# A chain of norms, mixers and experts on one core: Flow's entry reordered, stage changes keyed to the last products, filler moved

## The chip, the core and the metric

The kernel runs on one core of one Trainium2 chip. Its engines are PE (TensorE: matrix products and transposes), DVE (VectorE), ACT (ScalarE), POOL (GpSimd) and SP, which here issues the DMAs. Each engine runs its own instructions in the order in which they are written and waits on semaphores for the others. The metric is the device time of one execution in microseconds; lower is better. The time before is 947.53 us, the median of 3 runs (947.06 to 948.75).

## What is computed

x is 4096 tokens of 128 channels (4 sequences of 1024). Six blocks follow one another, each on the layer norm of x, each added to x:

```python
x = x + 0.5 * ffn0(norm(x))       # stage 1: silu(gate) * up, hidden 384
x = x + time_mixing(norm(x))      # stage 2: a decayed scan over time
x = x + 0.5 * ffn0(norm(x))       # stage 3
x = x + 0.5 * experts(norm(x))    # stage 4: 8 experts, top 2, gelu
x = x + flow(norm(x))             # stage 5: causal "flow" attention, 16 heads of 8
x = x + 0.5 * experts(norm(x))    # stage 6
```

Flow is what the change is mostly about:

```python
q, k = sigmoid(x @ Wq + bq), sigmoid(x @ Wk + bk); v = x @ Wv + bv
sink   = n / sum_d((q + eps) * (cumsum(k) + eps))            # first sum
source = n / sum_d((k + eps) * (cumsum(q) + eps))
con_sink   = sum_d((q + eps) * (cumsum(k * source) + eps)) / n   # second sum
con_source = sum_d((k + eps) * (cumsum(q * sink) + eps)) / n
cs = exp(con_source); comp = cs / cumsum(cs) * n             # third sum
out = (q * sink / n) . cumsum(k (x) v * comp) * sigmoid(con_sink)
out @ Wo + bo
```

## The kernel before

x stays in SBUF as X, 32 tiles of 128 tokens. Each stage runs over 8 chunks (NCH) of four tiles, 512 tokens, pipelined by hand: every engine has its own program text with the same stages, and `stages` strings them together with a wait at each change. FF, TM, MO and FL are the semaphore sets of ffn0, time mixing, experts and Flow.

At a stage change ACT writes the first chunk's normalised input Z "ahead" of the wait. PE then turns it (`turn_chunk`, four 128-wide transposes into a bank of PSUM), and ACT copies the turned tile to SBUF, from where PE multiplies. Before, the wait between the two stages was on `x` of the old stage, which DVE counts up when it has added the stage's last chunk to X (`add_to_x`, L1241); in the text it is, for the change from stage 4 to Flow, `eng.wait_ge(MO.x, NCH + CREDIT)`. The semaphores `down`, `out` and `rT` of the change are PE's own: they count its last transposes or projections of a chunk, which DVE's addition reads. POOL's `ahead` for Flow fills the carries cum1 and cum2 of the sums behind the same wait (L749 to L751).

In Flow the engines go through i = -1 to 8 and work in step i on chunk a = i + 1 (first part), b = i (second part) and c = i - 1 (last part). On PE a step is, in its order: `turned_output`, `states`, `project` of earlier chunks; `turn_chunk(a)`; `second_sum(b)`; `queries_keys(a)`; `values(a)`; a product of 64 columns over cs (third sum, L1898); `first_sum(a)`; the turn of qq (L1916) and more states. In step 0 the order is another: `queries_keys(1)` and `values(1)` come ahead of `second_sum(0)`, since nothing older is there to be done.

A running sum over a chunk is two carried products (the last row of the previous sums, `carried`, 128x512, weight last_row) and two running products (triangular weight until, `running`). second_sum(b) waits for w2, which POOL makes (L830) from DVE's reciprocals of the first sum; DVE's row products (L1452, L1454) read it; from these ACT makes cs (L1082) and a sigmoid (L1088, with a table load ahead of it); PE's small product over cs, DVE's L1482 to L1490, and POOL's kc and qq (L830) follow, then POOL's four key-value products a chunk (L823), which PE's `states` sum up (L1787) and DVE multiplies in `turn` (L1441, L1446) by the query.

`keep_busy(n, to)` issues n fillers, products whose result nobody reads (L1614), into bank `to`. `variances` (L1218 to L1228) is DVE's statistics for the next stage; it is seven small instructions, and at Flow's end it stands between DVE's turns of chunk 6 and of chunk 7.

In the profile the 512-wide and 128-wide fp32 products have two records each, so "x4" of a 512-wide one is two products. All products of Flow that go through `add` carry the line L1780.

## Time and profile before

| | us |
|---|---|
| median of 3 runs (lowest, highest) | 947.53 (947.06, 948.75) |
| the profiled execution's own time | 946.31 |
| its span, first to last instruction | 944.6 |
| PE busy | 868.7 |
| DVE busy | 721.7 |
| ACT busy | 637.8 |
| POOL busy | 589.1 |

The mean granted clock of PE is 0.973 of full speed; in any short stretch it is either 1.00 (2.4 GHz) or 0.50 (1.2 GHz), and a number between them means that the stretch held both. Flow lies between about 510 and 714 us. A row of the timeline gives start, length, engine, source line, operation, output <- inputs, count, and in brackets how long the engine had stood still and what released it. Ends of PE's products are modelled, so the distance from one start to the next is the better measure of what a product costs.

### The profile page before, as it was taken

How to read it: one execution, taken by the hardware profiler on the slowest of the kernel's cores; microseconds unless marked ns; L12 is line 12 of the kernel's file. 1: busy time of each engine (PE TensorE's matmuls, PEld its weight loads, DVE VectorE, ACT ScalarE, POOL GpSimd, SP SyncE). 2: the span in 40 equal slices, each digit the busy share in tenths (PEclk: the TensorE clock that was granted, in tenths of full speed). 3: DMA queues.
4: the chain of work that ended last, by engine and by line, in shares of the span. 5: the costliest groups of instructions: out<-in, count | busy, mean ns of one | idle time of the engine just before them, and what ended most of it. 6: DMA issues, size and time to landing. Idle time of an engine off the chain costs nothing.

```text
span 944.6 us, 14308 instructions
## 1 busy us (share of the span) xinstructions
PE 868.7 (92%) x3982; PEld 465.1 (49%) x3982; DVE 721.7 (76%) x1541; ACT 637.8 (68%) x1153; POOL 589.1 (62%) x560
## 2 busy tenths in 40 slices
PE   7989897787987999999999899999987899999998
PEld 6845463344543444444444456666544444444443
DVE  6956669985676788888865488888886788888874
ACT  3078789977876887788885444444315878788884
POOL 2075775569567766666677355555474766666774
PEclk9999979889999999999999999999989999999999
DMA  8000000000002222211220000000002232123230
GB/s 227 12 1 0 0 1 1 0 1 1 1 1 90 90 91 91 90 55 47 77 91 0 0 2 0 1 1 1 0 1 90 90 93 58 64 89 101 101 102 23
DMA packets 27407, 42.12 MB, mean 45 GB/s; under 512 B 5320, under 2 KB 19036, under 8 KB 27356
## 3 DMA queue, kind: packets, MB, share of 16 engines
q1 hardware_dynamic: 27356, 41.52, 13.8%
q8 instruction: 22, 0.36, 0.2%
q14 instruction: 29, 0.24, 0.1%
HBM read 39.15 MB, written 2.36 MB: 44 GB/s over the span
## 4 chain that ended last, share of the span: by engine, by line
PE 54%; DVE 22%; issue 9%; ACT 8%; POOL 4%; DMA 1%; DVEq 1%; SPq 1%; ACTq 0%; POOLq 0%
PE bank L1780 11%; PE bank L1525 10%; PE bank L1527 9%; PE bank L1526 9%; PE bank L1787 5%; DVE arena L1367 3%; ACT bank L1016 3%; PE bank L1620 2%; POOL rstd L718 1%; PE bank L1747 1%; DVE arena L1414 1%; DVE arena L1413 1%; ACT arena L1008 1%; DVE stats L1199 1%; DVE arena L1441 1%
## 5 line engine op out<-in xcount | busy, mean ns | idle before, releaser
L805 POOL TENSOR_TENSOR arena<-arena 128x512 f16<-128x512 f32 x256 | 293.3, 1159 | 127.0 <-ACT arena L1008 126.2
L1367 DVE TENSOR_TENSOR arena<-bank,arena 128x512 f32<-128x512 f32 x256 | 172.9, 686 | 75.7 <-ACT bank L1016 59.0
L1008 ACT ACTIVATE arena<-arena 128x512 f16<-128x512 f32 x256 | 160.6, 627 | 77.3 <-DVE arena L1367 76.0
L1016 ACT ACTIVATE bank<-bank,eb 128x512 f32<-128x512 f32 x256 | 166.3, 654 | 9.2 <-PE bank L1527 8.7
L1525 PE MATMUL bank<-arena,ew1hi 128*128 128x512 f16 x256 | 97.6, 381 | 1.9 <-DVE arena L1367 1.9
L1526 PE MATMUL bank<-arena,ew1hi 128*128 128x512 f16 x256 | 97.8, 382 | 0.0
L1527 PE MATMUL bank<-arena,ew1lo 128*128 128x512 f16 x256 | 97.7, 382 | 0.0
L1525 PE MATMUL bank<-arena,ew2hi 128*128 128x512 f16 x256 | 97.5, 381 | 0.0
L1526 PE MATMUL bank<-arena,ew2hi 128*128 128x512 f16 x256 | 97.5, 381 | 0.0
L1527 PE MATMUL bank<-arena,ew2lo 128*128 128x512 f16 x256 | 97.5, 381 | 0.0
L830 POOL TENSOR_TENSOR arena<-arena 128x512 f32<-128x512 f32 (+1 forms) x24 | 32.8, 1379 | 86.4 <-DVE arena L1485 65.9
L771 POOL TENSOR_TENSOR arena<-arena 128x512 f16<-128x512 f32 x46 | 52.9, 1161 | 41.1 <-ACT arena L934 41.1
L1787 PE MATMUL bank<-arena,until 128*128 128x512 f32 x128 | 63.7, 621 | 4.3 <-DVE arena L1441 4.2
L1525 PE MATMUL bank<-arena,f0hi 128*128 128x512 f16 x144 | 54.7, 380 | 8.0 <-DVE arena L1270 2.6
L823 POOL TENSOR_TENSOR arena<-arena 128x1024 f32<-128x1024 f32 x32 | 61.7, 1951 | 0.0
L1270 DVE SCALAR_TENSOR_TENSOR arena<-bank,arena 128x512 f32<-128x512 f32 x48 | 33.0, 691 | 28.4 <-ACT arena L943 22.7
L1527 PE MATMUL bank<-arena,f0lo 128*128 128x512 f16 x144 | 54.6, 379 | 0.0
L1526 PE MATMUL bank<-arena,f0hi 128*128 128x512 f16 x144 | 54.6, 379 | 0.0
L920 ACT ACTIVATE Z<-X,nbias,rstd 128x128 f32<-128x128 f32 (+1 forms) x128 | 52.4, 483 | 1.1 <-POOL pool_spare L720 1.1
L1380 DVE TENSOR_SCALAR X<-X,keep,shift (+1 forms) x64 | 51.7, 812 | 0.0
L1441 DVE TENSOR_TENSOR arena<-bank,arena 128x512 f32<-128x512 f32 x64 | 41.9, 684 | 7.5 <-PE bank L1787 7.5
L1199 DVE BATCH_NORM_STATS2 stats<-X 128x6 f32<-128x128 f32 (+1 forms) x188 | 43.6, 286 | 4.7 <-issue 1.5
(278 smaller groups left out, 1850.0 us busy)
## 6 DMA issues: line engine op xcount, KB each, us to landing
arena<-wrows SPq DMA_DIRECT2D x64, 512.0 KB, 5.9
X<-in_L_attn_x_dram SPq DMA_DIRECT2D x8, 256.0 KB, 4.3
out_dram<-X SPq DMA_DIRECT2D x8, 256.0 KB, 5.6
arena<-in_L_ffn_ew_dram SPq DMA_DIRECT2D x2, 512.0 KB, 6.6
arena<-in_L_ffn_ew_dram SPq DMA_DIRECT2D x1, 1024.0 KB
wrows<-arena SPq DMA_DIRECT2D x16, 16.0 KB
arena<-in_L_ffn_gens_dram SPq DMA_DIRECT2D x1, 192.0 KB, 2.6
arena<-in_L_ffn_w_gate_dram SPq DMA_DIRECT2D x1, 192.0 KB, 2.8
```

The source lines that it names most:

```text
L771: pool.tensor_tensor(f0.hlo[:, u, :], f0.h[:, u % 2, :], f0.hhi[:, u, :], ALU.subtract).then_inc(S.hlo, 1)
L805: pool.tensor_tensor(mo.hlo[:, u % 8, :], mo.hw[:, u % 4, :], mo.hhi[:, u % 8, :], ALU.subtract).then_inc(S.hlo, 1)
L823: pool.tensor_tensor(fl.kv[:, b, :].rearrange("p (h m d) -> p h m d", d=HD, m=HD), key.to_broadcast([P, HEADS, HD, HD]), value.to_broadcas ...
L1008: A(mo.hhi[:, u % 8, :], mo.hw[:, u % 4, :], ACT.Copy).then_inc(S.hhi, 1)
L1016: A(bank[MM1_BANK[u]][:, :], bank[MM1_BANK[u]][:, :], ACT.Gelu, scale=1.0 / WS, bias=eb1[:, u:u + 1]).then_inc(S.gelu, 1)
L1199: last = dve.bn_stats(stats[:, bass.ds(tile, 1), :], X[:, bass.ds(tile * P, P)])
L1367: TT(mo.hw[:, u % 4, :], bank[MM1_BANK[u]][:, :], mo.wB[:, p, u // EB, :], ALU.mult)\
L1525: mm(dst, whi, xhi, start=start, stop=False, skip_group_check=True)
L1526: mm(dst, whi, xlo, start=False, stop=False, skip_group_check=True)
L1527: return mm(dst, wlo, xhi, start=False, stop=stop, skip_group_check=True)
L1780: return mm(dst, w, x, start=start, stop=stop, skip_group_check=True)
L1787: mm(bank[5 + h], until[:, :], fl.kv[:, b, h * CH:(h + 1) * CH], start=True, stop=True)\
```

## The change

It has four parts.

1. Flow, step 0 on PE: the carried products of `second_sum` become a function of their own, `second_carry`. In step 0 it stands ahead of `turn_chunk(1)`, in all later steps where it was. `values(1)` moves from ahead of the second sum to behind the small product over cs. Of the fillers around the first two chunks the seven at the end of step -1 and the two of step 0 go, and eight new ones follow `values(1)`. On ACT `value_copy(1)` moves from behind the gates to behind the sigmoid of the second sum, as in the other steps.
2. On PE and ACT (`products=True`) the wait at each of the five stage changes is for the old stage's last product on PE, no longer for DVE's addition to X. POOL's wait ahead of the fills of cum1 and cum2 changes in the same way. Two waits that this needs are put further on: `S.init` in time mixing, and in the first experts stage a wait for FF.x ahead of the gate products, whose bank DVE still reads.
3. Flow, step 7 on PE: the eight fillers ahead of the turn of qq go; four come ahead of the small product over cs, and six behind it.
4. The nine fillers in the first step of an experts stage write bank 2, not bank 0.

```diff
@@ stages @@
-        def stages(eng, ffn0, mixing, experts, flow, ahead):
+        def stages(eng, ffn0, mixing, experts, flow, ahead, products=False):
...
             ahead(TM, 0, 2)
-            eng.wait_ge(FF.x, NCH + CREDIT)
+            if products:
+                eng.wait_ge(FF.down, NCH)
+            else:
+                eng.wait_ge(FF.x, NCH + CREDIT)
             mixing(TM, 0, 2)
...
             ahead(FL, 0, 5)
-            eng.wait_ge(MO.x, NCH + CREDIT)
+            if products:
+                eng.wait_ge(MO.rT, NCH)
+            else:
+                eng.wait_ge(MO.x, NCH + CREDIT)
             flow(FL, 0, 5)
             ahead(MO, NCH, 6)
-            eng.wait_ge(FL.x, NCH)
+            if products:
+                eng.wait_ge(FL.out, NCH)
+            else:
+                eng.wait_ge(FL.x, NCH)
             experts(MO, NCH, 6)
@@ gpsimd, ahead @@
                     if number == 5 and n == 2:
-                        pool.wait_ge(MO.x, NCH + CREDIT)
+                        pool.wait_ge(MO.rT, NCH)
@@ scalar, flow @@
                     if i == 0:
                         gates(a)
-                        value_copy(a)
...
-                    if a < NCH and i != 0:
+                    if a < NCH:
                         value_copy(a)
@@ tensor, mixing @@
             def mixing(S, first, number):
-                pe.wait_ge(S.init, 1)
...
                         o = p * CH
+                        if not lead:
+                            pe.wait_ge(S.init, 1)
                         pe.wait_ge(S.xn, i + 3)
@@ tensor, experts @@
                             if mid:
                                 pe.wait_ge(S.wT, i + 1)
+                            elif number == 4:
+                                pe.wait_ge(FF.x, 2 * NCH + CREDIT)
...
                             if not mid:
-                                keep_busy(9, 0)
+                                keep_busy(9, 2)
@@ tensor, flow @@
-                def second_sum(b):
+                def second_carry(b):
 
                     after(pe, S.snap2, b)
                     after(pe, S.qqT, b)
...
                     for m in range(2):
                         carried(3, m, fl.cum2)
+
+                def second_sum(b):
+
                     pe.wait_ge(S.w2, b + 1)
...
                         project(c - 1)
+                    if i == 0:
+                        second_carry(b)
                     if a < NCH:
                         after(pe, S.pr, a)
                         after(pe, S.snap1, a)
                         turn_chunk(Z, a % 2, S.z, a + 1, S.tr, 1)
                     if i == 0:
-                        keep_busy(2, 5)
                         queries_keys(a)
-                        values(a)
+                    if now and b:
+                        second_carry(b)
                     if now:
                         second_sum(b)
...
                     if a < NCH and i != 0:
                         values(a)
+                    if i == NCH - 1:
+                        keep_busy(4, 1)
                     if now:
                         pe.wait_ge(S.cs, b + 1)
...
                         last.then_inc(S.ccp, 1)
+                    if i == 0:
+                        values(a)
+                        keep_busy(8, 5)
+                    if i == NCH - 1:
+                        keep_busy(6, 1)
                     if a < NCH and i != 0:
                         first_sum(a)
-                    if i < 0:
-                        keep_busy(7, 5)
                     if 0 <= c:
                         states(c, 3)
                     if now:
-                        if i == NCH - 1:
-                            keep_busy(8, 1)
                         pe.wait_ge(S.qq, b + 1)
```

PE's instructions from the end of the first chunk's first sum on, before. last_row is a carried product, until a running one, fw with 256 columns queries and keys, fw with 128 columns values, f0hi a filler, ident with Z the turn.

```order
L1614 MATMUL bank<-f0hi 128x512 x7
L1620 MATMUL bank<-ident,Z 128x128 x4
L1614 MATMUL bank<-f0hi 128x512 x2
L1780 MATMUL bank<-bias_rows,ones 128x512
L1780 MATMUL bank<-fw,arena 128x256 x2
L1780 MATMUL bank<-bias_rows,ones 128x512
L1780 MATMUL bank<-fw,arena 128x256 x2
L1780 MATMUL bank<-bias_rows,ones 128x512
L1780 MATMUL bank<-fw,arena 128x128 x4
L1780 MATMUL bank<-arena,last_row 128x512 x2
L1780 MATMUL bank<-arena,until 128x512 x2
```

Behind them come the first sum of the second chunk (two carried, two running products), the small product over cs and the turn of qq. The same place on PE after the change, up to values:

```order
L1796 MATMUL bank<-arena,last_row 128x512 x2
L1634 MATMUL bank<-ident,Z 128x128 x4
L1796 MATMUL bank<-bias_rows,ones 128x512
L1796 MATMUL bank<-fw,arena 128x256 x2
L1796 MATMUL bank<-bias_rows,ones 128x512
L1796 MATMUL bank<-fw,arena 128x256 x2
L1796 MATMUL bank<-arena,until 128x512 x2
L1796 MATMUL bank<-arena,last_row 128x512 x2
L1796 MATMUL bank<-arena,until 128x512 x2
L1921 MATMUL bank<-arena,until 128x64
L1796 MATMUL bank<-bias_rows,ones 128x512
L1796 MATMUL bank<-fw,arena 128x128 x4
```

The two carried products of the second sum have taken the place of the seven fillers, the running ones stand right behind queries and keys, and values (the last two rows) behind the small product over cs; eight fillers follow them, then the turn of qq.

PE's instructions in Flow's last full step (i = 7), before: states of chunk 6 (until, L1787), the two small products of the third sum (64 columns), states, fillers, the turn of qq, states of chunk 7.

```order
L1787 MATMUL bank<-arena,until 128x512 x2
L1898 MATMUL bank<-arena,until 128x64
L1901 MATMUL bank<-arena,last_row 128x64
L1787 MATMUL bank<-arena,until 128x512 x2
L1614 MATMUL bank<-f0hi 128x512 x8
L1916 MATMUL bank<-ident,arena 128x128 x4
L1787 MATMUL bank<-arena,until 128x512 x2
```

And after the change:

```order
L1803 MATMUL bank<-arena,until 128x512 x2
L1628 MATMUL bank<-f0hi 128x512 x4
L1921 MATMUL bank<-arena,until 128x64
L1924 MATMUL bank<-arena,last_row 128x64
L1628 MATMUL bank<-f0hi 128x512 x6
L1803 MATMUL bank<-arena,until 128x512 x2
L1940 MATMUL bank<-ident,arena 128x128 x4
L1803 MATMUL bank<-arena,until 128x512 x2
```

The fillers have moved from behind the last states of chunk 6 to both sides of the small products.

## Rows read from the trace of the kernel before

**Rows 1.** The page, first part: engine, busy us, share, instructions.
```profile
PE 868.7 (92%) x3982; PEld 465.1 (49%) x3982; DVE 721.7 (76%) x1541; ACT 637.8 (68%) x1153; POOL 589.1 (62%) x560
```

**Rows 2.** The chain of waits, 500 to 560 us: start us, length us, what.
```profile
513.27 7.44 PE bank L1780 x27
...
524.54 10.31 PE bank L1780 x35
```

**Rows 3.** Timeline, change into Flow: start, length, engine, what [idle <- releaser].
```profile
507.99 1.64 ACT L920 ACTIVATE Z<-X,nbias,rstd 128x128 f32<-128x128 f32 x4
...
509.58 0.65 PE L1756 MATMUL bank<-ident,arena 128*128 128x128 f32 x4 [0.92 <-DVE arena L1393]
...
511.02 0.97 PE L1620 MATMUL bank<-ident,Z 128*128 128x128 f32 x4 [0.78 <-DVE X L1241]
...
516.20 1.09 ACT L1055 ACTIVATE arena<-bank 128x512 f32<-128x512 f32 x2 [2.22 <-PE bank L1780]
```

**Rows 4.** Busy time by stretch (PEclk third number from the end).
```profile
511.00:515.00 4.00, 3.98 (x13) 2.64 (x14) 2.04 (x11) 1.88 (x2) 3.76 (x5) 0.57 0.00 0
538.30:542.00 3.70, 3.70 (x14) 3.02 (x15) 1.82 (x3) 0.82 (x2) 3.70 (x3) 0.54 0.00 0
688.50:695.50 7.00, 5.24 (x8) 1.93 (x9) 5.94 (x10) 0.86 (x3) 6.20 (x5) 0.52 0.02 4
560.00:680.00 120.00, 118.02 (x506) 72.06 (x505) 100.60 (x150) 51.75 (x85) 62.71 (x38) 1.00 0.00 1
```

**Rows 5.** The timeline, Flow's second chunk.
```profile
520.54 1.67 PE L1614 MATMUL bank<-f0hi 128*128 128x512 f16 x7
...
523.22 0.63 PE L1620 MATMUL bank<-ident,Z 128*128 128x128 f32 x4 [1.00 <-issue]
...
524.54 0.39 PE L1780 MATMUL bank<-bias_rows,ones 128*128 128x512 bf16 x1 [0.26 <-ACT arena L1073]
...
524.80 1.97 POOL L830 TENSOR_TENSOR arena<-arena 128x1024 f32<-128x1024 f32 x1 [5.92 <-DVE arena L1511]
...
526.91 1.09 ACT L1055 ACTIVATE arena<-bank 128x512 f32<-128x512 f32 x2 [2.42 <-PE bank L1780]
526.92 1.05 PE L1780 MATMUL bank<-fw,arena 128*128 128x128 f32 x8
...
529.53 1.88 PE L1780 MATMUL bank<-arena,until 128*128 128x512 f32 x4
```

**Rows 6.** The timeline, from the wait for qq to the third turn.
```profile
538.16 3.85 POOL L823 TENSOR_TENSOR arena<-arena 128x1024 f32<-128x1024 f32 x2
...
538.25 0.90 PE L1916 MATMUL bank<-ident,arena 128*128 128x128 f32 x4 [3.23 <-POOL arena L830]
...
544.98 0.60 PE L1620 MATMUL bank<-ident,Z 128*128 128x128 f32 x4
```

**Rows 7.** The timeline, Flow's end.
```profile
690.26 3.75 PE L1787 MATMUL bank<-arena,until 128*128 128x512 f32 x4 [1.96 <-DVE arena L1441]
...
691.44 7.67 POOL L823 TENSOR_TENSOR arena<-arena 128x1024 f32<-128x1024 f32 x4
...
694.05 0.69 DVE L1441 TENSOR_TENSOR arena<-bank,arena 128x512 f32<-128x512 f32 x1 [0.89 <-PE bank L1787]
...
695.92 1.35 DVE L1218 TENSOR_TENSOR halfd<-stats 128x24 f32<-128x24 f32 x1
...
697.19 1.99 DVE L1219 TENSOR_TENSOR var<-stats 128x24 f32<-128x24 f32 x1
...
700.76 1.96 PE L1787 MATMUL bank<-arena,until 128*128 128x512 f32 x4 [0.27 <-DVE arena L1441]
```

**Rows 8.** The timeline at the change into the second experts stage.
```profile
714.84 0.66 PE L1620 MATMUL bank<-ident,Z 128*128 128x128 f32 x4 [0.78 <-DVE X L1241]
...
716.78 0.69 DVE L1372 TENSOR_TENSOR arena<-bank,arena 128x512 f16<-128x512 f32 x1
```

**Rows 9.** The timeline at the change into the first experts stage.
```profile
281.50 0.63 PE L1620 MATMUL bank<-ident,Z 128*128 128x128 f32 x4 [0.54 <-ACT Z L920]
```

More of the change, by code:

```diff
@@ L534, in stages @@
             ahead(TM, 0, 2)
-            eng.wait_ge(FF.x, NCH + CREDIT)
+            if products:
+                eng.wait_ge(FF.down, NCH)
+            else:
+                eng.wait_ge(FF.x, NCH + CREDIT)
             mixing(TM, 0, 2)
             ahead(FF, NCH, 3)
-            eng.wait_ge(TM.x, NCH + CREDIT)
+            if products:
+                eng.wait_ge(TM.out, NCH)
+            else:
+                eng.wait_ge(TM.x, NCH + CREDIT)
             ffn0(FF, NCH, 3)
             ahead(MO, 0, 4)
-            eng.wait_ge(FF.x, 2 * NCH + CREDIT)
+            if products:
+                eng.wait_ge(FF.down, 2 * NCH)
+            else:
+                eng.wait_ge(FF.x, 2 * NCH + CREDIT)
             eng.wait_ge(S0.flo, NU // TILES + 1)
@@ L545, in stages @@
             ahead(FL, 0, 5)
-            eng.wait_ge(MO.x, NCH + CREDIT)
+            if products:
+                eng.wait_ge(MO.rT, NCH)
+            else:
+                eng.wait_ge(MO.x, NCH + CREDIT)
             flow(FL, 0, 5)
             ahead(MO, NCH, 6)
-            eng.wait_ge(FL.x, NCH)
+            if products:
+                eng.wait_ge(FL.out, NCH)
+            else:
+                eng.wait_ge(FL.x, NCH)
             experts(MO, NCH, 6)
@@ L1106, in _ @@
             setup()
-            stages(act, ffn0, mixing, experts, flow, ahead)
+            stages(act, ffn0, mixing, experts, flow, ahead, products=True)
         @block.vector
@@ L1932, in _ @@
             setup()
-            stages(pe, ffn0, mixing, experts, flow, lambda S, first, number: None)
+            stages(pe, ffn0, mixing, experts, flow, lambda S, first, number: None, products=True)
 _INS = ["L0_attn_x", "L0_attn_time_decay", "L0_attn_time_first", "L0_attn_time_mix_k", "L0_attn_time_mix_v",
```

## The prediction

> **What bounds the kernel now.** I read the page first: PE is busy 92% of the span [rows 1], so what can be won lies where PE stands still, runs at half clock, or does on the path what could stand elsewhere. Then the chain of waits around Flow's entry (500 to 560 us). It is PE almost throughout; two long pieces, 513.27 to 520.71 and 524.54 to 534.85, hold the first chunk's and the second chunk's products in a row [rows 2]. Between 560 and 680 us PE is busy 118.02 of 120 us [rows 4], so what is saved at the entry is handed on. Then the timeline at the stage change [rows 3], the granted clock by stretch [rows 4], the timeline of the second chunk [rows 5, 6], Flow's end [rows 7] and the other changes [rows 8, 9]. The reader should see in them who is last at each step.
>
> **Stage changes.** Five times PE and ACT no longer wait for DVE's last addition to X but for PE's own last product. It is worth something only where Z, which ACT writes ahead, is already there.
> Into Flow it is: Z is written by 509.63, PE's last transposes end at 510.23, and PE starts the turn at 511.02, after DVE's addition [rows 3]. It can now start at about 510.3: 0.7 us. There is a second gain behind it. The clock was half from 511 to 515 (0.57) [rows 4], after PE had stood for 0.92 and 0.78 us [rows 3]. Without the second pause I expect it to stay full. At full clock the second chunk's step from turn to query-key products takes 524.54 - 523.22 = 1.32 us and from there to ACT's gates 526.91 - 524.54 = 2.37 us [rows 5]. The first chunk's gates so start at 510.3 + 1.32 + 2.37 = 513.99 and not at 516.20 [rows 3]: **2.2 us**, bounds 0.7 (clock falls all the same) and 2.3. What follows the gates was a closed PE chain [rows 2] and moves along. POOL's two fills of the carries move with the same wait and stay ahead of their reader.
> Into the second experts stage the turn at 714.84 could start at most 0.78 us sooner. But the next on the path is DVE's residual of xn at 716.78, which DVE starts without a pause, right behind its own work on the last chunk [rows 8], and that still waits for the last projection: 0. At the other three changes (there are three such rows, one is shown) it is ACT's Z, not DVE's addition, that PE waited for [rows 9]. I take 0 for them, bounds 0 and 0.2 in all. The new wait of the first experts stage's gate products for X stands behind ACT's copy and holds nobody; what is queued behind it on PE is filler.
>
> **The second sum.** From the first to the second chunk the path is turn, query-key products, values, carried products, running products, then DVE's row products, two running products (1.72 us) after 529.53 [rows 5]. The change takes two pieces out: values and the two carried products, together the 2.8 us from 526.75 (values' bias product stands just ahead of the row at 526.92) to 529.53; 1.72 of it is the carried ones, two of 0.86 us, so 1.1 is values. The carried ones go into the hole where PE ran seven fillers (1.67 us from 520.54) while it waited for ACT's copy of the first sum [rows 5]; they take as long, so they are done by 522.4 and the turn still starts at 523.22: cost 0. The running products need w2, which POOL finishes at 524.80 + 1.97 = 526.77 [rows 5]; PE gets there at 526.75. So they start at 526.85 instead of 529.53: **2.7 us** (2.6 to 2.8). This price rests on POOL: any further cut before it is worth nothing.
> Values now stand behind the small product over cs. cs comes 2.7 us earlier as well, since ACT then waits for nothing but DVE's row products. The first sum of the second chunk ends on PE at 534.85 - 2.7, still just where cs is ready. Then PE waited 3.23 us for POOL's qq until 538.25 [rows 6]; that wait is as long as before, since DVE, ACT and POOL between cs and qq are not changed. Values (1.1 us) and eight fillers (1.7 us) lie in that wait, together 2.8, so cover remains, 0.4 us. If it were gone they would cost what they overrun. ACT now copies the values between its sigmoid and its copy of the third sum, so its copy of the first sum comes about 0.6 us later relative to the rest; its reader on PE is the next turn, behind four 512-wide products: 0.
>
> **The clock behind the hole.** After those 3.23 us PE's clock was 0.54 until 542 [rows 4]. The turn of qq, the eight small products and the first states took 538.25 to 544.98 [rows 6]. With the hole filled, PE starts the first states as soon as POOL's first product is there, 538.16 + 1.92 = 540.1, and the second pair when POOL's second ends, 542.0; two products of 0.86 us each end at about 543.8, and the next turn starts then: **1.15 us**, bounds 0.4 and 1.2. Again POOL is the limit. Later the loop is PE's, so it stays.
>
> **Flow's end.** Eight fillers go from behind the last states of chunk 6 to before (4) and behind (6) the small product over cs of the last chunk. The places were pauses (1.96 us in the second [rows 7]); after them the clock was 0.52 from 688.5 to 695.5 [rows 4] and the two products of the states took 3.75 us, where two take 1.88 to 1.96 at full clock [rows 5, 7]. DVE waited 0.89 us there, at 694.05. That wait goes, but buys nothing. DVE's next work is the seven statistics instructions of the next stage, and their first two, on 24 elements a partition, take 1.35 and 1.99 us; they end at 697.27 and 699.18, both just behind a boundary of POOL's four 1.92 us products (691.44 to 699.11) [rows 7]. POOL is not moved, so its last product ends at 699.11 and I let DVE get through behind it as before, at best one instruction sooner: 0.1 us. The Trainium skill states the mechanism (page "SBUF — State Buffer", section "Who interferes with whom"): a DVE instruction with two SBUF inputs contends with a GpSimd instruction that reads SBUF, and the later one waits for the whole of the other. By that rule DVE stays pinned; without it the 0.9 us would come through.
> PE, however, is now early: at full clock its states of chunk 6 end at 692.0, the turn of qq at 692.5, the first states of chunk 7 at 695.1 (they wait for POOL at 693.4), the turned output at 696.9. The next states need DVE's first turn of chunk 7, 700.6 as now (PE started at 700.76) [rows 7]. A pause of 3.7 us opens that the late fillers used to close (0.27 us now). The pause of 3.23 us before 538.25 was followed by half clock for some 3.5 us [rows 4, 6]. The same here makes 3.4 to 3.7 us of PE work take 1.7 us more; DVE's chain of four turns has about 0.35 us of slack for it. Cost **+1.3 us**; bounds -0.9 (clock holds and DVE is not pinned) and +2.8 (half clock for 7 us, as from 688.5).
>
> **The sum.** -2.2 - 2.7 - 1.15 - 0.1 + 1.3 = -4.85; I say -4.8. The span goes from 944.6 to 939.8, the profiled execution's time from 946.31 to 941.5; the median of the three runs is 1.2 above the profiled time, so 947.53 - 4.8 = 942.7. About 0.2% (1.9 us) is what a measurement of this kernel can tell from no change.
>
> **Rivals.**
> 1. Flow's end costs nothing or gains, because the pause falls so that the clock holds, or DVE passes between POOL's products: sum -6.1 to -7.0, time 940.5 to 941.4. For it: one execution does not tell where the fall lands against the pause. Against: the one pause above 3 us in these rows was followed by it at once [rows 4, 6]. 0.2.
> 2. The clock still falls at Flow's entry, since the 0.92 us pause stays: first term 0.7, sum -3.3, time 944.2. 0.14.
> 3. Flow's end costs the double, half clock over two turns: sum -3.3, time 944.2. 0.1.
> 4. It does not do what it says: w2 or qq is later than read, so values or fillers overrun and the second term halves: sum -3.4, time 944.1. 0.04.
> 5. Slower. The entry loses its fillers: PE stands from 522.4 to 523.2 and again from the turn's end to 524.54, and if that drops the clock to half from 524.5 on, each 3.5 us of PE work there costs 1.75. It decides from about 7 us on: with 10 us of work at half clock +5, first term 0.7, third 0, end +2.8: -0.7 - 2.7 + 5 + 2.8 = +4.4, time 951.9. Against: together these pauses are under 1.6 us, with full work between and behind. 0.04.
> My forecast 0.48.
>
> **The numbers.** Forecast 942.7; the range 940.3 to 945.0 takes in rivals 1 to 4 and leaves out the slower one and the far ends of the others. Faster by over 0.2% (below 945.6): 0.93; within 0.2%: 0.04; slower: 0.03.
>
> **What the profile after would show.** Right: PE's turn into Flow right behind its own transposes and a clock of 1.00 up to the gates; DVE's row products of the second sum about 4.9 us earlier than now; no half clock behind the qq wait; at Flow's end DVE's second statistics instruction still ending with a POOL product, PE standing over 3 us before the second states of the last chunk, then half clock. Wrong: the turn waits for Z or the clock drops at 511; the running products start well after the query-key products; DVE's statistics end earlier than POOL's last product, or no half clock after 700, then the gain is larger; the loop between 560 and 680 longer than its present chunk.

## The result and the profile after

The changed kernel takes 942.23 us (median of 4 runs, 940.39 to 943.67), the kernel before 947.60 beside it (median of 4, 947.06 to 948.75): ratio 0.9943, 95% interval 0.9924 to 0.9961, so 5.4 us less (3.7 to 7.2). The forecast was 942.7, -4.8 us, with the range 940.3 to 945.0. The profiled execution after took 943.67 us with a span of 941.9.

PE's busy time fell by 1.5 us, its span in these two executions by 2.7. The page after, against [rows 1]:

```profile
PE 867.2 (92%) x3983; PEld 461.9 (49%) x3983; DVE 722.8 (77%) x1541; ACT 637.5 (68%) x1153; POOL 588.6 (62%) x560
```

At the change into Flow, the timeline after (start, length, engine, what [idle <- releaser]), against [rows 3]:

```profile
511.68 0.66 PE L1772 MATMUL bank<-ident,arena 128*128 128x128 f32 x4 [0.92 <-DVE arena L1407]
512.37 0.69 DVE L1255 SCALAR_TENSOR_TENSOR X<-bank,X 128x512 f32<-128x512 f32 x1 [0.75 <-PE bank L1772]
...
512.40 0.66 PE L1634 MATMUL bank<-ident,Z 128*128 128x128 f32 x4
...
513.15 0.60 ACT L1088 ACTIVATE arena<-bank 128x512 f32<-128x512 f32 x1 [1.42 <-PE bank L1634]
...
516.17 1.08 ACT L1070 ACTIVATE arena<-bank 128x512 f32<-128x512 f32 x2 [1.12 <-PE bank L1796]
```

PE's transposes for DVE start at 511.68 and the turn of the first chunk stands 0.72 us behind them, with no idle time; before it was 1.44 us behind, 0.78 of it waiting for DVE's addition. The gates at 516.17 stand 3.80 us behind the start of DVE's addition (512.37), before 5.93 (510.27 to 516.20): -2.13 us.

The second chunk, against [rows 5, 6]:

```profile
520.52 1.88 PE L1796 MATMUL bank<-arena,last_row 128*128 128x512 f32 x4
...
523.19 0.63 PE L1634 MATMUL bank<-ident,Z 128*128 128x128 f32 x4 [0.80 <-issue]
...
524.77 1.97 POOL L845 TENSOR_TENSOR arena<-arena 128x1024 f32<-128x1024 f32 x1 [4.52 <-DVE arena L1525]
...
526.79 1.98 PE L1796 MATMUL bank<-arena,until 128*128 128x512 f32 x4
...
528.82 1.22 DVE L1466 SCALAR_TENSOR_TENSOR arena<-arena,bank 128x1024 f32<-128x1024 f32 x1 [4.22 <-PE bank L1796]
...
532.43 1.05 PE L1796 MATMUL bank<-fw,arena 128*128 128x128 f32 x8
...
533.32 1.89 PE L1628 MATMUL bank<-f0hi 128*128 128x512 f16 x8
...
535.61 0.66 PE L1940 MATMUL bank<-ident,arena 128*128 128x128 f32 x4 [0.40 <-POOL arena L845]
...
537.52 3.96 PE L1803 MATMUL bank<-arena,until 128*128 128x512 f32 x8 [0.36 <-POOL arena L838]
...
541.32 0.60 PE L1634 MATMUL bank<-ident,Z 128*128 128x128 f32 x4
```

The carried products (last_row, 520.52) fill the hole ahead of the turn, the running ones start at 526.79, just as POOL's w2 is there (524.77 + 1.97 = 526.74). PE's wait for qq is down from 3.23 to 0.40 us, and the third turn follows 28.92 us behind the first, before 33.96.

Flow's end, against [rows 7], and the turn into the second experts stage, against [rows 8]:

```profile
686.60 1.95 PE L1803 MATMUL bank<-arena,until 128*128 128x512 f32 x4 [0.66 <-DVE arena L1455]
...
687.78 7.66 POOL L838 TENSOR_TENSOR arena<-arena 128x1024 f32<-128x1024 f32 x4
...
689.78 1.98 PE L1803 MATMUL bank<-arena,until 128*128 128x512 f32 x4 [0.79 <-POOL arena L838]
...
691.27 0.42 DVE L1232 TENSOR_TENSOR halfd<-stats 128x24 f32<-128x24 f32 x1
...
691.62 1.98 DVE L1233 TENSOR_TENSOR var<-stats 128x24 f32<-128x24 f32 x1
...
693.52 1.98 DVE L1235 SCALAR_TENSOR_TENSOR nmean<-stats 128x24 f32<-128x24 f32 x1
...
696.97 2.66 PE L1803 MATMUL bank<-arena,until 128*128 128x512 f32 x4 [3.42 <-DVE arena L1455]
...
702.59 0.69 DVE L1455 TENSOR_TENSOR arena<-bank,arena 128x512 f32<-128x512 f32 x1 [0.98 <-PE bank L1803]
...
711.96 0.69 DVE L1255 SCALAR_TENSOR_TENSOR X<-bank,X 128x512 f32<-128x512 f32 x1 [2.61 <-PE bank L1796]
...
712.26 0.63 PE L1634 MATMUL bank<-ident,Z 128*128 128x128 f32 x4 [0.34 <-ACT Z L935]
...
714.52 0.69 DVE L1386 TENSOR_TENSOR arena<-bank,arena 128x512 f16<-128x512 f32 x1
```

The states of chunk 6 take 1.95 us and no more 3.75. DVE's statistics (L1232 to L1242) still end with POOL's products: these are four of 1.92 us from 687.78, with boundaries at 689.70, 691.61, 693.53 and 695.44, and L1233 and L1235 end at 693.60 and 695.50. PE stands 3.42 us ahead of the next states, which then take 2.66 instead of 1.95. And the clock by stretch, against [rows 4] (length, busy time and records of PE, PEld, DVE, ACT, POOL, then PEclk):

```profile
511.00:515.00 4.00, 3.15 (x17) 2.08 (x18) 2.90 (x13) 2.56 (x4) 2.46 (x4) 1.00 0.00 0
535.00:543.00 8.00, 7.22 (x28) 3.85 (x28) 6.56 (x9) 3.18 (x6) 8.00 (x5) 1.00 0.01 2
688.00:691.00 3.00, 2.21 (x9) 1.14 (x8) 2.97 (x5) 0.60 (x1) 3.00 (x2) 1.00 0.01 3
698.00:701.50 3.50, 3.50 (x12) 2.23 (x11) 3.07 (x4) 0.00 (x0) 2.98 (x10) 0.51 0.00 0
```

Full where it was half before (511 to 515, 538 to 542, from 688.5), and half in a new place, 698 to 701.5.

### The profile page after: what moved, and what is told of

It reads as the page before. It is cut to its first block, busy times and chain, and to the rows that moved or that the text cites. A ratio compares the mean times of both kernels' runs of the same rounds, so it can differ in the third digit from the quotient of the medians.

```text
span 941.9 us, 14312 instructions
## 1 busy us (share of the span) xinstructions
PE 867.2 (92%) x3983; PEld 461.9 (49%) x3983; DVE 722.8 (77%) x1541; ACT 637.5 (68%) x1153; POOL 588.6 (62%) x560
## 4 chain that ended last, share of the span: by engine, by line
PE 52%; DVE 21%; issue 10%; ACT 8%; POOL 7%; DMA 1%; DVEq 1%; SPq 1%; ACTq 0%; POOLq 0%
PE bank L1796 11%; PE bank L1539 9%; PE bank L1540 9%; PE bank L1541 9%; PE bank L1803 4%; DVE arena L1381 3%; ACT bank L1031 3%; POOL rstd L733 2%; PE bank L1634 1%; PE bank L1763 1%; DVE arena L1428 1%; ACT arena L1023 1%; DVE arena L1427 1%; DVE arena L1455 1%; DVE stats L1213 1%
```

## What every trace shows, side by side

Each experiment left a trace, and the same marks can be read in each: "entry" is from DVE's last addition of stage 4 to POOL's first key-value product of Flow's last chunk, "end" from there to DVE's last addition of Flow. From the third turn to that product it is 146.45 to 146.47 us in every one of the 14 traces, so all differences of the entry lie ahead of the third turn. The turns of the first, second and third chunk lie within the entry. From DVE's last addition of Flow to the end of the span it is 229.7 to 231.7 us in all of them, whatever the kernel.

| kernel | first to second turn | first to third | entry | end |
|---|---|---|---|---|
| before | 12.20 | 33.96 | 181.17 | 22.65 |
| before again (e8) | 12.21 | 34.08 | 181.29 | 22.64 |
| before, third (e9) | 10.79 | 33.69 | 180.90 | 22.63 |
| after | 10.79 | 28.92 | 175.41 | 24.18 |
| after again (e5) | 10.79 | 28.92 | 175.42 | 22.52 |
| after, third (e10) | 10.80 | 28.92 | 175.40 | 24.18 |
| entry alone (e1) | 10.80 | 28.93 | 176.13 | 22.53 |
| stage changes alone (e2) | 10.79 | 32.45 | 178.94 | 24.19 |
| end fillers alone (e3) | 10.80 | 33.70 | 180.92 | 25.56 |
| after without the eight (e4) | 10.80 | 28.92 | 175.40 | 24.18 |
| pause filled (e6) | 10.79 | 28.91 | 175.40 | 22.53 |
| statistics early (e7) | 10.80 | 28.91 | 175.40 | 18.86 |
| before, statistics early (e11) | 10.80 | 33.76 | 180.96 | 21.01 |
| e7 without end fillers (e12) | 10.79 | 28.91 | 175.39 | 20.48 |

The profiled execution after had lost time before Flow began: DVE's first addition to X lies at 67.78 us, in the one of before at 64.88. Of these 2.9 us 1.2 were lost in the set-up (the products behind PE's pause of 2.63 us there start at 59.68 and not at 58.47) and 1.7 to the clock behind that pause, which was 0.57 from 59.5 to 63.5, where it was 1.00 before: to the next turn PE takes 4.93 us instead of 3.24. The change doesn't touch this part. The same late start is in e2 (67.75) and in e8, the kernel before itself (67.88), and in none of the other ten traces of an experiment (64.76 to 65.39); the pause stands in all 14. Of the 2.9 us 2.1 are left where Flow begins. So the two profiled executions (946.31 and 943.67) differ by -5.76 us in the entry, +1.53 at Flow's end, +2.1 ahead of Flow and -0.5 behind it, together -2.6. The medians carry the result.

A second thing can be read from the 14 traces. With the entry in the old order (before, e8, e9, e2, e3, e11) the clock falls behind the wait for qq in all six; in the new order (after, e5, e10, e1, e4, e6, e7, e12) it falls there in none of the eight.

## Experiments: the parts one by one

The first four ran beside the kernel before (947.63 us, 31 runs).

**e1, Flow's entry alone** (part 1; the waits put further on and part 4 stay in). The stage changes and the fillers of Flow's end are as before. The edit is against the kernel after:

```diff
-                        pool.wait_ge(MO.rT, NCH)
+                        pool.wait_ge(MO.x, NCH + CREDIT)
...
-            stages(act, ffn0, mixing, experts, flow, ahead, products=True)
+            stages(act, ffn0, mixing, experts, flow, ahead)
...
-                    if i == NCH - 1:
-                        keep_busy(4, 1)
...
-                    if i == NCH - 1:
-                        keep_busy(6, 1)
...
+                        if i == NCH - 1:
+                            keep_busy(8, 1)
...
-            stages(pe, ffn0, mixing, experts, flow, lambda S, first, number: None, products=True)
+            stages(pe, ffn0, mixing, experts, flow, lambda S, first, number: None)
```

> The kernel before with part 1 of the change alone (carried products ahead, values behind the small product over cs, eight fillers behind them); waits at the stage changes and fillers at Flow's end as before. My theory: from PE's first turn in Flow to its third (33.96 us before, 28.92 after) it takes 2.7 us less for the second sum and 1.1 less for the clock, 30.1 us, and the time is 3.8 us below before. Rival (the shortened path runs into another wait that the stage change also had to move): the stretch stays above 31.5 and the time falls by 2 us or less.

Measured: 943.71 us (12 runs), ratio 0.9960 (0.9947 to 0.9974), -3.8 us by the ratio. The entry is 176.13 us, 4.8 to 5.2 shorter than in the three traces of before, and 0.73 longer than in after. First to third turn takes 28.93 us, as in after, where I expected 30.1; the rival (above 31.5) is out. Its profiled execution was the fastest of the twelve (939.60), so the trace says what the part can give in a good one (4.8 to 5.2 us) and the median what it gave (2.5 to 5.0 us by the interval). What the stage change adds in these traces is 0.73.

**e2, the stage changes alone** (parts 2 and 4): the entry and Flow's end in the order of before. The edit against after, shortened; the fillers of Flow's end (4 and 6 back to 8) and ACT's `value_copy` go back as well.

```diff
-                    if i == 0:
-                        second_carry(b)
...
                     if i == 0:
+                        keep_busy(2, 5)
                         queries_keys(a)
-                    if now and b:
+                        values(a)
+                    if now:
                         second_carry(b)
...
-                    if i == 0:
-                        values(a)
-                        keep_busy(8, 5)
...
+                    if i < 0:
+                        keep_busy(7, 5)
```

> The kernel before with the waits at the five stage changes alone. My theory: only the change into Flow pays; from PE's last transposes of the experts stage (509.58 before) to ACT's first gates (516.20 before) 6.62 us become 4.5, and the time falls by 2.1 us. Rival (the clock falls at Flow's entry whatever the wait): 0.7 us. Second rival (the other four changes pay too, 0.5 us each): over 3.5 us.

Measured: 944.84 us (11 runs), ratio 0.9974 (0.9957 to 0.9991), -2.5 us by the ratio. The entry is 178.94, 2.0 to 2.35 less than before: 0.73 from the turn and the rest from the clock, which in this execution fell for less time behind the wait for qq than in e9: first to third turn takes 32.45 us, in the five traces with the old wait and the old order 33.69 to 34.09. From PE's last transposes (511.20) to the first gates (515.70) it is 4.50 us, as expected. The rival of 0.7 us lies just outside the interval (0.9 to 4.1 us less); the one of over 3.5 us is not shut out by it, but first addition to last of stage 4 shows nothing of it (below). Flow's end cost 24.19 here, though its fillers stand as before (PE's timeline):

```profile
689.66 1.95 PE L1804 MATMUL bank<-arena,until 128*128 128x512 f32 x4 [1.95 <-DVE arena L1456]
...
700.04 2.38 PE L1804 MATMUL bank<-arena,until 128*128 128x512 f32 x4 [2.76 <-DVE arena L1456]
```

The states of chunk 6 run at full clock (1.95 us), so PE is early and stands for 2.76 us, and the states behind that take 2.38. So with the fillers in their old place, too, half clock can follow a pause ahead of these states.

**e3, the end fillers alone** (part 3), on the kernel before:

```diff
+                    if i == NCH - 1:
+                        keep_busy(4, 1)
                     if now:
                         pe.wait_ge(S.cs, b + 1)
...
+                    if i == NCH - 1:
+                        keep_busy(6, 1)
...
-                        if i == NCH - 1:
-                            keep_busy(8, 1)
```

> The kernel before with the fillers of Flow's last full step moved alone. My theory: slower by 1.4 us than before; DVE's statistics still end with POOL's last product, PE then stands over 3 us and runs its next states and the projection at half clock. From POOL's first key-value product of the last chunk (691.44 before) to DVE's last addition to X in Flow (714.09 before) 22.65 us become 24.1. Rival (the move keeps the clock up and DVE gains its wait): 0.9 us faster than before, 21.8.

Measured: 948.84 us (11 runs), ratio 1.0015 (0.9999 to 1.0030), +1.4 us by the ratio. The pause is 3.42 us as in after, and here the states behind it ran wholly at half clock (PE's timeline):

```profile
690.04 1.95 PE L1787 MATMUL bank<-arena,until 128*128 128x512 f32 x4 [0.66 <-DVE arena L1441]
...
700.41 3.75 PE L1787 MATMUL bank<-arena,until 128*128 128x512 f32 x4 [3.42 <-DVE arena L1441]
```

3.75 us for what takes 1.95, and the end 25.56 us, 2.9 over before, where I expected 24.1. By its interval (-0.1 to +2.8 us) the time is barely apart from no change; the rival, 0.9 us faster, is out. The sum of the three parts by their ratios, -3.8 - 2.5 + 1.4 = -4.9, stands beside -5.4 for the whole: they add up within their intervals, which are wide (1.3 to 1.8 us to each side). By the traces the entry alone and the stage changes alone save more together (4.8 to 5.2 and 2.0 to 2.35) than the two in one kernel (5.5 to 5.9): a part of the clock's share is in both.

**e4, after without the eight fillers** behind values:

```diff
                     if i == 0:
                         values(a)
-                        keep_busy(8, 5)
```

> The changed kernel without the eight fillers behind the values of the second chunk. My theory: PE stands 2.1 us ahead of the turn of qq, then runs at half clock, and the first states come late: the third turn 1.1 us later than in the changed kernel (28.92 us after the first turn there), 30.0, and the time 1.1 us above it. Rival (values alone hold the clock, the gain of the third term is the reordering's): no difference, 28.9.

Measured: 942.28 us (9 runs), ratio 0.9948 (0.9932 to 0.9965), and first to third turn 28.92 us, the same as with them. PE stands longer, and no half clock follows (PE's timeline):

```profile
532.61 0.66 PE L1939 MATMUL bank<-ident,arena 128*128 128x128 f32 x4 [2.12 <-POOL arena L845]
```

The fillers do nothing that a trace or the time shows. My theory, which gave them the third term, missed, and the rival was right: values' place, with which the wait is 2.12 us and not 3.23, is enough.

## Experiments: the clock, from one execution to the next

**e8 and e9, the kernel before again, and e10 and e5, after again.** Nothing is edited.

> The kernel before, unchanged, for a second trace of it. It tells whether the half clock from 511 to 515, to which my first term gave 1.4 of its 2.2 us, belongs to the kernel or to one execution: in four traces of other kernels with the old wait or the old order since, PE's first turn in Flow to its second took 10.8 us and not 12.2. My theory now: 10.8, so that the stage change was worth 0.7 us and not 2.2 in most executions. Rival (the 0.78 us pause causes the fall): 12.2 again.

> The kernel before, unchanged, a third trace, with the same two readings: first turn in Flow to second 10.8 (theory now) or 12.2 (rival). And from first turn to third: 33.7 or less, with half clock behind the wait for qq, whose length differs from trace to trace.

> The changed kernel, unchanged, a third trace. At Flow's end one trace of it had half clock behind the pause and took 24.18 us from POOL's first key-value product of the last chunk to DVE's last addition, the other had none and took 22.52, with the same pause of 3.42 us. Theory: it is the execution that decides, so either value and none between; PE's first turn in Flow to its third 28.92 in any case. Rival (the third term depends on the execution as well): 30 or more in one of the traces.

> The changed kernel once more, unchanged, for a second trace of it on one chip with the runs beside it: 942 to 943 us. It tells whether the 2.9 us by which the profiled execution of the changed kernel was already late at DVE's first addition to X (67.78 against 64.88) belong to the change. My theory: they belong to the execution; a second trace has that addition anywhere between 64.5 and 68. Rival (the moved waits or the larger program make the set-up longer): again 67.5 or more.

Measured: e8 949.62, e9 945.12 and e10 941.40 (one run each; 946.53 is the median of 15 runs of before beside them), e5 942.90 (6 runs, beside 948.45), ratio 0.9945 (0.9924 to 0.9966). That is the result of the change once more. e5's first addition to X lies at 65.39 us, so the late start isn't the change's. e8 has 12.21 us from first to second turn, the rival's number and not my 10.8; e9 has 10.79. e10 gave 24.18, one of the two values that I expected, and 28.92.

The windows of e9, the kernel before, show the half clock in another place than I had read it:

```profile
511.00:515.00 4.00, 3.67 (x22) 2.82 (x21) 1.52 (x8) 2.61 (x4) 3.71 (x8) 1.00 0.00 0
535.00:543.00 8.00, 6.68 (x18) 4.11 (x18) 4.36 (x6) 2.19 (x4) 8.00 (x6) 0.57 0.01 2
```

The turn waited for DVE as before (PE's timeline):

```profile
510.50 0.66 PE L1620 MATMUL bank<-ident,Z 128*128 128x128 f32 x4 [0.78 <-DVE X L1241]
```

The same wait of 0.78 us, and the clock stays at full speed from 511 to 515. The first to second turn takes 10.79 us, 1.4 less than in the first trace. Of six traces with the old stage change (before, e8, e9, e3, e11, e1) two show the fall at 511 and four don't. In e9 the half clock is all behind the wait for qq instead (0.57 over 8 us, before 0.79), and the third turn comes nearly as late (33.69 and 33.96). So the two stretches trade: in all five traces with the old wait and the old order (these three, e3, e11) first to third turn takes 33.69 to 34.09 us, however the half clock is shared between them. The entry is 180.90 to 181.29 in the three traces of before, and 175.40 to 175.42 in the three of after. None of the eight traces with the new wait has the fall at the turn; with two of six on the other side that may be the shorter pause or chance.

At Flow's end the same holds for after. e5 has the same pause, in PE's timeline:

```profile
694.96 1.96 PE L1803 MATMUL bank<-arena,until 128*128 128x512 f32 x4 [3.43 <-DVE arena L1455]
```

and no fall behind it, by the window:

```profile
695.00:703.00 8.00, 7.56 (x25) 3.42 (x25) 7.80 (x11) 0.00 (x0) 7.07 (x15) 1.00 0.00 0
```

Behind 3.42 or 3.43 us of pause the states took 2.66 us (after), 2.52 (e10), 2.46 (e4), 3.75 (e3) and 1.96 (e5). The end follows: 24.18 three times, 25.56, and 22.52.

**e6, the pause filled.** Fourteen fillers in PE's pause of step 8:

```diff
+                    if i == NCH:
+                        keep_busy(14, 2)
                     if 0 <= c:
                         states(c, 1)
```

> The changed kernel with 14 fillers in PE's pause at Flow's end, between the turned output of chunk 6 and the second states of chunk 7. My theory (the pause costs the clock, and the clock costs 1.4 us): the granted clock stays at 1.00 until Flow's last addition, the stretch from POOL's first key-value product of the last chunk (687.78) to DVE's last addition (711.96), 24.18 us in the changed kernel, becomes 22.7, the time 1.4 us less. Rival (DVE's late statistics alone make the end, PE only follows): 24.2 as before it, no difference.

Measured: 940.41 us (5 runs), ratio 0.9926 (0.9903 to 0.9948), beside 942.90 for e5 on the same chip. PE's timeline:

```profile
691.06 3.19 PE L1628 MATMUL bank<-f0hi 128*128 128x512 f16 x14
694.66 1.95 PE L1803 MATMUL bank<-arena,until 128*128 128x512 f32 x4 [0.41 <-DVE arena L1455]
```

The pause shrinks to 0.41 us and the end is 22.53, the value of e5 without a fall. The interval overlaps that of e5, and e5's trace had no fall either, without fillers. So e6 is in line with my theory, that the pause costs the clock (it fell behind it in four of the five traces in which it stood), but one trace doesn't prove it.

## Experiments: who holds Flow's end

**e7, the statistics one step earlier.** In the prediction DVE's statistics were pinned by POOL's products. They need only the first six chunks' additions, and can stand in step 7 behind the row products, ahead of POOL's key-value products:

```diff
-                    if b == NCH:
-                        variances(number + 1, False)
...
+                    if b == NCH - 1:
+                        variances(number + 1, False)
```

> The changed kernel with DVE's seven statistics instructions for the next stage moved one step ahead, to where DVE waits 1.13 us for the small product over cs and POOL stands still. My theory (POOL's products hold back three of the seven): they take about 1.0 us there, DVE's first turn of chunk 7 starts 4.5 us earlier, PE has no long pause, and the end of Flow comes 4 to 5 us earlier; time 4.5 us below the changed kernel. Rival (the statistics only fill time that DVE has anyway, since it waits for POOL's key-value products, the last of which ends at 695.44): 2 us or less.

Measured: **936.87 us** (5 runs, 936.44 to 937.95), ratio 0.9882 (0.9864 to 0.9900). That is 6.0 us under e5 on the same chip, the intervals don't touch, and it is faster than both kernels. Timeline:

```profile
681.07 0.19 DVE L1232 TENSOR_TENSOR halfd<-stats 128x24 f32<-128x24 f32 x1
681.18 0.19 DVE L1233 TENSOR_TENSOR var<-stats 128x24 f32<-128x24 f32 x1
...
681.29 0.20 DVE L1235 SCALAR_TENSOR_TENSOR nmean<-stats 128x24 f32<-128x24 f32 x1
...
685.39 7.67 POOL L838 TENSOR_TENSOR arena<-arena 128x1024 f32<-128x1024 f32 x4
...
690.99 1.88 PE L1803 MATMUL bank<-arena,until 128*128 128x512 f32 x4
...
692.05 0.69 DVE L1455 TENSOR_TENSOR arena<-bank,arena 128x512 f32<-128x512 f32 x1 [0.64 <-PE bank L1803]
```

The three instructions that take 0.42, 1.98 and 1.98 us in after take 0.19, 0.19 and 0.20 here. DVE then reaches its turn of chunk 7 while POOL still works, PE has no pause, and the end is 18.86 us: 5.3 less than after, 3.7 less than e5 (I expected 4 to 5).

**e11, the same edit on the kernel before.**

> The kernel before with DVE's seven statistics instructions one step ahead, nothing else of the change. My theory: POOL's products held the statistics back in the kernel before as well, so the gain does not hang on the change: from POOL's first key-value product of the last chunk to DVE's last addition 22.65 us become 19 to 20 (the late fillers and their half clock are still there), the time 3 us or more below before. Rival (the pause that the change opened is what the move closes): under 1 us.

Measured: 945.60 us (11 runs) beside 946.53 (15 runs), ratio 0.9999 (0.9981 to 1.0016). Of the gain of e7 nothing is left that the times show; in the trace the end is 21.01, 1.6 less. My theory wanted 3 us in the time, and 19 to 20 us for the end; the time is the rival's. The timeline shows why it was missed:

```profile
686.46 0.19 DVE L1218 TENSOR_TENSOR halfd<-stats 128x24 f32<-128x24 f32 x1
...
689.59 3.44 PE L1787 MATMUL bank<-arena,until 128*128 128x512 f32 x4 [1.95 <-DVE arena L1441]
...
692.86 1.89 PE L1614 MATMUL bank<-f0hi 128*128 128x512 f16 x8
...
695.03 1.88 PE L1787 MATMUL bank<-arena,until 128*128 128x512 f32 x4
...
696.09 0.69 DVE L1441 TENSOR_TENSOR arena<-bank,arena 128x512 f32<-128x512 f32 x1 [1.08 <-PE bank L1787]
...
699.59 0.69 DVE L1441 TENSOR_TENSOR arena<-bank,arena 128x512 f32<-128x512 f32 x1 [0.70 <-PE bank L1787]
```

DVE's statistics are short here too, but PE is late: the states of chunk 6 take 3.44 us at half clock, the eight fillers (1.73 us to the next start) stand ahead of the turn of qq and of the first states of chunk 7, and DVE waits for PE 1.08 and 0.70 us. The old place of the fillers cost nothing as long as DVE was held anyway. With DVE free it is on the path. So part 3, which alone costs 1.4 us, seems to be what makes room for e7. That is read from this trace: no run has the whole change with the eight fillers in their old place.

**e12, e7 without the ten fillers of step 7.** The edit against e7:

```diff
-                    if i == NCH - 1:
-                        keep_busy(4, 1)
...
-                    if i == NCH - 1:
-                        keep_busy(6, 1)
```

> The changed kernel with DVE's seven statistics instructions one step ahead, as in the version that measured 936.87, and with no fillers at all in Flow's last full step (neither the four nor the six). It asks what part 3 of the change gives once DVE is freed. My theory: without them PE stands 1.23 and 1.96 us around the small product over cs, half clock falls on the states that follow in part of the executions, DVE waits for them, and the stretch from POOL's first key-value product of the last chunk to DVE's last addition is 19.5 to 21 us in such a trace, 18.9 in one without; the time 0.5 to 1.5 us above 936.9. Rival (these fillers do nothing, it was only their old place that cost): 18.9 and 936.9.

Measured: 937.44 us (4 runs), ratio 0.9888 (0.9856 to 0.9921). PE's timeline:

```profile
683.99 3.75 PE L1803 MATMUL bank<-arena,until 128*128 128x512 f32 x4 [1.95 <-DVE arena L1455]
687.54 1.06 PE L1936 MATMUL bank<-ident,arena 128*128 128x128 f32 x4
```

Without fillers the states of chunk 6 take 3.75 us again, the turn of qq 1.06, and the end 20.48, 1.6 over e7. That is within what I expected (19.5 to 21), but the times don't separate the two (0.9888 and 0.9882), so the rival, that these fillers do nothing for the time, stays open. What e7 gains over after comes from the statistics; what the ten fillers add to it is at most these 1.6 us of one trace, and not shown by the times.

## Why the prediction was right, and where its steps were not

**The sum.** -4.8 us forecast, -5.4 measured (3.7 to 7.2 less). By the traces the entry gives -5.5 to -5.9 and the end +1.5 or -0.1 by execution, where I had -6.05 and +1.2. So the mechanisms of the entry and of the pinned statistics were right. That the sum comes this close is in part luck: two terms had a wrong cause or place (below), and the end is either of two values by execution.

**Stage change into Flow, -2.2.** In the first trace of each kernel it is -2.13, turn and clock as worked out. But the step "without the second pause I expect it to stay full" took one execution's half clock for the kernel's: with the pause the clock stays full as well in four of six traces. The 0.73 us of the turn is in every trace: PE's first turn starts 0.75 us behind the start of DVE's last addition in the six with the old wait, 0.02 in the eight with the new. The clock's share isn't lost for nothing, since in the old order what isn't lost here is lost behind the wait for qq: e2, the stage changes alone, saves 2.0 to 2.35 us of the entry and 2.5 in time (0.9 to 4.1). In the new order of the entry that second place is gone, and e1 against after leaves 0.73. The right form of the term would have been 0.7 for the turn and the clock's share counted once for both places.

**The other four stage changes, 0.** DVE's residual of the second experts stage (L1386) stands 2.56 us behind DVE's last addition (711.96 to 714.52), before 2.69 (714.09 to 716.78): 0.13 us. From the first addition to the last of stage 4 it is 444.4 to 445.4 us in the traces of before and 444.6 to 445.1 in those of after: nothing to be seen of the three changes in front. At the first experts stage PE waits for Z as before [rows 9]:

```profile
283.73 0.52 PE L1634 MATMUL bank<-ident,Z 128*128 128x128 f32 x3 [0.53 <-ACT Z L935]
```

**The second sum, -2.7.** Right in each part: the carried products fit into the hole, the turn still follows after 0.80 us of issue, the running ones start 0.05 us behind POOL's w2. DVE's row products come 16.45 us behind the last addition of stage 4, before 21.18: -4.73 for the -4.9 of the first two terms. Values overran nothing, and the wait for qq kept 0.40 us of cover, as the prediction had it. The row of before:

```profile
531.45 1.22 DVE L1452 SCALAR_TENSOR_TENSOR arena<-arena,bank 128x1024 f32<-128x1024 f32 x1 [6.82 <-PE bank L1780]
```

**The clock behind the qq wait, -1.15.** The third turn comes 5.76 us earlier against the addition, for 6.05 forecast, so the term was 1.0 here. In e9 and e3, where the half clock lay wholly behind that wait, the term is 2.1 (33.7 to 28.9, less 2.7). That the new order ends this half clock is shown (six of six traces against none of eight). The cause in the prediction was wrong in part: not the hole filled with fillers (e4), but values and the shorter wait.

**DVE's statistics, -0.1.** Right: the 0.9 us of DVE's wait for PE brought nothing. They were even held once more than before, L1235 too. The Trainium skill has the mechanism (page "SBUF — State Buffer", section "Who interferes with whom"): a DVE instruction with two inputs in SBUF contends with a GpSimd instruction that reads SBUF, and the later one waits for the whole of the other. The traces agree: the same instruction takes 1.98 us beside POOL's products and 0.19 without them. What I missed is that this hold cost more at Flow's end than the clock (1.7 us in after), and that a step of seven small instructions could be moved from under it: e7 shows 3.7 to 5.3 us.

**Flow's end, +1.3.** The pause of 3.7 us was 3.42, half clock followed, and the end grew by 1.53 us. But rival 1 (the clock holds) is not a rival so much as another execution: e5 has it. In the medians both are mixed: the end fillers alone cost 1.4 us (-0.1 to +2.8). The part that was not foreseen is that the old place has the same risk once the clock has not fallen earlier (e2).

**Rivals.** 1 is told above. 2 (the clock falls at the entry all the same) is in none of the traces of after; 3 (double cost) not in after, but in e3; 4 and 5 did not occur: e4 takes the remaining fillers of the entry away and the time is the same.

**Open** is what decides in which execution the clock falls; no run was made for it. Open too is what bounds e7's end now; in the turns of chunk 7 its trace has PE and DVE one after the other, with waits of DVE of 0.17 to 0.64 us. And the profiled executions are single ones: the kernel before took 943.2 to 950.0 us over all its runs, more than the whole gain, so a part of a microsecond is told by the traces and not by the times.

## What to carry to other kernels

Where a small DVE step with SBUF inputs stands beside long POOL products, look at its mean duration against the same step elsewhere: the seven took 5.0 us here and 1.2 in e7, and once the change was in, moving them by one step of the loop was worth as much again as all its four parts (6.0 and 5.4 us), while on the kernel before it gave nothing that the times show. Take a half-clock stretch of one trace as belonging to that execution until a second trace has it in the same place, and count what it costs once, over the whole stretch in which it may fall. Fillers are free only while another engine holds the path; check them again when that engine is relieved.

## What was unexpected of the hardware

The same kernel had its half-clock stretches in different places: the kernel before behind the turn into Flow in two of three executions (0.57 from 511 to 515 in the first), the kernel after behind its 3.42 us pause in two of three, and three of fourteen traces had one at 59.5 to 63.5, behind a pause of 2.63 us that stands in all of them. Such a stretch cost 1.4 us at the turn into Flow, 1.7 at 59.5, and 1.7 to 3.0 at Flow's end (24.18 and 25.56 against 22.52). The length of a pause didn't decide: the clock fell behind one of 0.78 us in two traces and held behind one of 3.43 in another. The Trainium skill says (page "TensorE: Matmul & The Clock Gate", part 1) that the activity monitor runs freely and that for the first switch of a kernel the moment so differs from run to run; this is in line with the traces, but none of them shows the cause.

POOL's products, back to back, let exactly one held DVE instruction through per product: in after L1232, L1233 and L1235 end at 691.69, 693.60 and 695.50, POOL's boundaries being 691.61, 693.53 and 695.44. DVE's instructions behind them, of one SBUF input or after POOL's last product, take 0.18 us each.
